# Second attention: weighings 6 and 7 of a batch issued back to back, the next batch's first folded context behind them

## The reference, cut to what matters

```
q = (x @ Wq).reshape(b, n, H, DH)              # H = 16 heads of DH = 64
k = (context @ Wk * SCALE).reshape(b, m, H, DH)
v = (context @ Wv).reshape(b, m, H, DH)
scores = einsum('bihd,bjhd->bhij', q, k)
attn = softmax(scores, axis=-1)
out = einsum('bhij,bjhd->bihd', attn, v).reshape(b, n, H * DH)
x = x + tanh(g_xattn[1]) * (out @ Wo + bo)     # x before was layer-normed for q
```

## Time and profile before

| | |
|---|---|
| median of 3 runs | 806.19 us (805.4 to 810.56) |
| profiled execution, its own time | 808.45 us |
| its span in the profile | 806.7 us |
| granted TensorE clock, mean | 0.997 |
| matmul busy | 767.2 us, 95% |
| weight loads busy | 630.8 us, 78% |
| VectorE busy | 617.2 us, 77% |
| ScalarE busy | 548.6 us, 68% |
| GpSimd busy | 464.7 us, 58% |

### The profile page before, as it was taken

One profiled execution on the slowest core, in us unless ns is written; L12 is line 12 of the kernel. 1 busy time (PEld: TensorE's weight loads), 2 busy tenths in 40 slices (PEclk: granted clock), 3 DMA queues, 4 the chain that ended last, 5 costly groups with the idle time before them and its releaser, 6 DMA issues. The chain is left out here.

```text
span 806.7 us, 30355 instructions
## 1 busy us (share of the span) xinstructions
PE 767.2 (95%) x10573; PEld 630.8 (78%) x10573; DVE 617.2 (77%) x2395; ACT 548.6 (68%) x1107; POOL 464.7 (58%) x868
## 2 busy tenths in 40 slices
PE   4999999999999989999999999999999999889996
PEld 2777777777788868888888888888888888548885
DVE  5899999998777777788787887888878887735543
ACT  2787887886455568777777777777777776147772
POOL 4555777772012156576677676776767766314554
PEclk9999999999999999999999999999999999999998
DMA  7905999600200000000000000000000000023100
GB/s 234 297 4 179 276 256 241 143 1 3 73 1 0 0 1 3 2 8 7 7 0 7 7 7 7 0 7 7 7 7 3 3 7 8 11 68 95 35 29 19
DMA packets 56320, 41.69 MB, mean 52 GB/s; under 512 B 3929, under 2 KB 51811, under 8 KB 56016
## 3 DMA queue, kind: packets, MB, share of 16 engines
q1 hardware_dynamic: 52416, 36.32, 17.2%
q0 software_dynamic: 2272, 4.27, 1.6%
q10 hardware_dynamic: 1584, 0.47, 0.3%
HBM read 18.07 MB, written 23.44 MB: 51 GB/s over the span
## 5 line engine op out<-in xcount | busy, mean ns | idle before, releaser
L1674 PE MATMUL l_pv<-l_Z,l_probs 128*128 128x129 f32 x1024 | 164.0, 283 | 3.0 <-ACT l_probs L1502 1.4
L1674 PEld LDWEIGHTS l_pv<-l_Z,l_probs 128*128 128x128 f32 x1024 | 138.3, 191 | 21.7 <-issue 5.2
L1435 POOL TENSOR_TENSOR l_qk_lo<-w,l_qk_hi 128x512 f16<-128x512 f32 x128 | 144.5, 1159 | 0.6 <-ACT l_qk_hi L1496 0.6
L1157 DVE SCALAR_TENSOR_TENSOR x_sb<-l_pv,l_inv,x_sb 128x128 f32 (+1 forms) x256 | 89.8, 351 | 33.7 <-DVE l_inv L1144 6.5
L1492 ACT ACTIVATE w<-l_qk_bank 128x512 f32<-128x512 f32 x124 | 74.1, 597 | 52.7 <-PE l_qk_bank L52 50.8
L52 PE MATMUL l_tz<-M,cT 128*128 128x512 f16 x384 | 104.1, 380 | 0.5 <-ACT l_Z L1507 0.2
L1502 ACT ACTIVATE l_probs<-l_b 128x512 f32<-128x512 f32 x128 | 72.7, 595 | 45.1 <-PE l_b L1640 44.3
L508 DVE TENSOR_REDUCE n_shared<-fold_bank 128x4 f32<-128x512 f32 x128 | 87.5, 684 | 9.4 <-PE fold_bank L731 9.3
L1134 DVE TENSOR_REDUCE l_neg_max<-l_a 128x4 f32<-128x512 f32 x128 | 83.3, 682 | 2.2 <-PE l_a L1618 2.1
L1496 ACT ACTIVATE l_qk_hi<-w 128x512 f16<-128x512 f32 x124 | 77.4, 624 | 1.1
L1507 ACT ACTIVATE l_Z<-l_tz 128x512 f32<-128x512 f32 x124 | 74.1, 597 | 4.6 <-PE l_tz L52 1.1
(11 more groups left out here) (287 smaller groups left out, 2280.3 us busy)
## 6 DMA issues: line engine op xcount, KB each, us to landing
expert_rows<-empty_row SPq DMA_DIRECT2D x8, 2178.0 KB, 23.6
x_sb<-expert_rows SPq DMA_DIRECT2D x36, 66.0 KB, 2.2
w<-in_L_ffn_w SPq DMA_DIRECT2D x1, 2048.0 KB, 9.2
x_sb<-in_x SPq DMA_DIRECT2D x3, 512.0 KB, 6.8
ctx_sb<-in_ctx SPq DMA_DIRECT2D x3, 512.0 KB, 7.9
w_raw<-in_L_ffn_gate_w SPq DMA_DIRECT2D x1, 1408.0 KB, 10.5
w_raw<-in_L_ffn_up_w SPq DMA_DIRECT2D x1, 1408.0 KB, 12.1
downT<-in_L_ffn_down_w SPq DMA_DIRECT2D x2, 512.0 KB, 4.2
```

The costliest lines, as they stand in the source:

```text
L1157: nc.vector.scalar_tensor_tensor(out=total, in0=O[:, h, 0:P], scalar=inv[:, j:j + 1], in1=total, op0=ALU.mult, op1=ALU.add).then_inc(summe ...
L1435: nc.gpsimd.tensor_tensor(qk_lo[:, w, m, Q * u:Q * u + Q].rearrange("p t n -> p (t n)"), qk[:, u, m, :], qk_hi[:, w, m, Q * u:Q * u + Q].r ...
L1674: last = nc.tensor.matmul(pv_bank[m % 2][:, h * (P + 1):(h + 1) * (P + 1)], probs[:, 2 * m + h, :], Z[:, w, 2 * m + h, :], start=True, sto ...
```

## The change

In every step of the second attention, TensorE's `weigh(n - 1, w, 7)` moves ahead of `project_context(f, w, 0)`, so that it stands directly behind `weigh(n - 1, w, 6)`; the context stands directly ahead of `score_by_key(n, u, 0)`. The conditions stay as they were: the weighing where there is a batch before, the context where there is a next batch. Nothing else changes.

```
                         transpose_maxima(n)
                         weigh(n - 1, w, 6)
+                    if not first:
+                        weigh(n - 1, w, 7)
                     if left:
                         project_context(f, w, 0)
-                    if not first:
-                        weigh(n - 1, w, 7)
                     score_by_key(n, u, 0)
                     if left:
                         score_by_query(f, w, 0)
```

## The result

The changed kernel takes 816.67 us (median of 6 runs, 814.11 to 818.52) against 807.06 for six runs of the kernel before. Compared side by side, round by round, the ratio is 1.0094 with a 95% interval of [1.0069, 1.012], or 7.6 us more. The forecast was 809.7, 3.5 us more, with a range up to 813.5: the sign was right, the forecast size was less than half of the measured one, and the range missed it. The profiled execution took 814.46 with a span of 812.7, 6.0 above that of before. Over the stretch of the loop, from the maxima's transpose of step 2 to that of step 31, the two traces differ by 7.62 us (366.99 against 359.37), so the loss lies there (outside it these two executions differ by 1.6 the other way).

The account below looks back on a forecast made before the run. TensorE, its matmul row occupied for the whole 24.8 us pass, was taken as the bound. The second steps' stall gave 808.45 + 3.5 = 812.0 for the profiled execution, 809.7 against the median, range 806.0 to 813.5.

Parts of the forecast that it names:

- Streaming: TensorE from weighing 6 to the scores: new order takes 1.77 against 1.75, counted as nothing, bounds 0 to +0.02.
- The wait of weighing 7 in the second steps: Second steps: weighing 7 waits for VectorE's sum of weighing 5, scores 0.25 us late; 14 × 0.25 = 3.5 us.
- ScalarE's copy of Z under cover: Behind the later context: ScalarE's copy still ends before the exponentials, 0.40 of cover in second steps; cost 0.
- VectorE hung on weighing 5: Second steps: VectorE's chain hangs on TensorE's weighing 5, a fixed 1.12 us, so the stall returns every pass.
- So I put the first steps at 0.: First steps of a pass: weighing 7's load only 0.03 late and covered, cost 0; without cover 0.4 us.
- has slack further on: First steps, weighing 2 to weighing 3: the transpose waits for GpSimd's normalised batch, 0.72 against 0.63, slack 0.09.
- (a): Rival, 10%: no stall, VectorE released earlier after the loop's jump; −1.2 us, 805.0 against the median.
- (b): Rival, 8%: the 0.25 is swallowed by a later TensorE wait on an engine not late; 806.2.
- (c): Rival, 8%: ScalarE's copy of Z decides the exponentials; +8.4 on top of 3.5, some 818.

Follow-up runs that it names:

- e2_first: The kernel before with the new order only in the first steps of a pass (u = 0); ratio 1.0004 to the kernel before.
- e10: The changed kernel with GpSimd's scatter by indirect DMA replaced by two tiny additions; ratio 1.0103 to the kernel before.
- e11: e4_variances with GpSimd's scatter by indirect DMA replaced by two tiny additions; ratio 1.0021 to the kernel before.
- e4_variances: The changed kernel with VectorE's two variance operations moved behind the sums of weighing 5 in first steps; ratio 1.0076 to the kernel before.
- e9_before_no_scatter: The kernel before with GpSimd's scatter by indirect DMA replaced by two tiny additions; ratio 0.9988 to the kernel before.
- e7: The kernel before with two passes written out per loop turn on all engines, 7 jumps instead of 14; ratio 1.0123.
- e1_second: The kernel before with the new order only in the second steps of a pass (u = 1); ratio 1.0074 to the kernel before.

## Why the prediction was wrong

- *Streaming*: right. e2_first has weighings 6 and 7, the context and the turn in 1.77 (loads at 497.72 and 499.49), 1.78 in most passes, with the 0.03 of wait in it.
- *The wait of weighing 7 in the second steps*: right to 0.01, mechanism, place and count: 14 × 0.247 = 3.46 against 3.5.
- *ScalarE's copy of Z under cover*, and *VectorE hung on weighing 5*: right (0.41 of cover, 1.12 of chain).
- **The step that failed: "So I put the first steps at 0."** It rested on the sum's end at 0.43 from the trace of before, as if only TensorE's order decided it. But the sums stand in VectorE's queue behind everything of the second step, and that had been shifted by the very stall that the forecast had worked out, against GpSimd, which had not shifted. The shift, 0.12 when it got there, made one product collide with GpSimd's fourth rest, cost 1.0 on VectorE, and left 0.27 at the sum. Measured in place of the 0: 0.27 in twelve first steps, 0.40 in step 4, 0.57 in step 30, 4.15 in all. e2_first shows that without the shift in the second steps the first steps are nearly free, e10 that the collision and its late sum make them dear with no hold about (12.93), e11 that they fall to 12.67 when the collision and the late sum are gone. That the margin was used up just so, to 0.01 us, is chance: in e4_variances, with a stall of 0.12 instead of 0.25, the product still starts 0.12 ahead of the rest and takes 0.19. A product left in front of the rest would have brought the number nearer to the forecast, with the same gap in the reasoning.
- *The remark that the first step "has slack further on"*: it gave back 0.03, not 0.09. In e9_before_no_scatter, where the batch is early, a first step is only 0.02 shorter.
- *The rivals*: none was it. (a) and (b) looked for something that swallows the stall, (c) for one that passes it on through ScalarE, and it was passed on through VectorE. The profile of before had a sign of it: the earlier trace rows count GpSimd as busy 17.65 of 24.83 us, and a product that starts 0.12 before a GpSimd instruction of 1.16 has 0.12 to spare against a stall of 0.25. A look at what stands on VectorE and GpSimd side by side behind the stall would have shown the risk, a possible 14 × 0.27 = 3.8 us, though hardly that half of the stall would be swallowed on the way.

Not settled: what the engines stand for behind the loop's jump; the trace has no row for it. In most first steps it takes both, the jump (e7) and the scatter (e9), but that is no full rule: in the kernel before, step 4, behind the first jump and the first scatter, has its cast at 0.52, and step 30, behind the loop, at 1.05. Nor is it settled why the scatter is done later in steps 4 and 30 of the changed kernel.

## What to carry to other kernels

When an edit delays one engine by a known amount, don't stop at the first wait that it lengthens: follow the delay through the queues of the engines that hang on it and look for places where it crosses the work of an engine that doesn't shift, above all VectorE instructions with two SBUF inputs beside long GpSimd ones. A margin smaller than the delay at its source (0.12 against 0.25 here) is a risk to be priced: what arrived was 0.12, it was enough, and it cost four times the stall on the spot. And a cure for one wait should be priced with the next one behind it in mind: e4_variances brought 1.3 us, and the same edit brings 5.6 once the hold behind it is gone.

## What the hardware showed

- A 128x16 product of VectorE that starts within 0.01 us of the start of a 128x512 instruction of GpSimd takes 1.19 us instead of 0.19, until 0.03 behind that instruction's end; in five kernels it ends 0.03 behind the rest in which it starts. GpSimd's instruction keeps its length (four in 4.52 us against 4.51).
- Behind this loop's jump, with an indirect DMA issued by GpSimd close by, VectorE or TensorE stood for 0.3 to 1.3 us without a semaphore that explains it. With the scatter's two parts at −1.00 and 0.38 around the step's start it is the cast (at 1.10 instead of 0.44), with −0.13 and 1.25 it is TensorE inside the scores in e1_second (0.27), and in the changed kernel, with the same two times, neither. In the three kernels that were run without the scatter nobody stands, and the kernel before is no faster for it (0.9988 [0.9966, 1.001]).
- This loop with a body twice as long pays more at its jump (first steps of 14.2 to 14.5 us against 12.66), enough to make halving their number a loss (1.0123 [1.0097, 1.0148]).
